# Quantized feed-forward block: scan and down stage in one block, other signed tiles, the first tile in four pieces

## The reference

```python
def act_qdq(x):
    qmax = 2.0 ** (ACT_BITS - 1) - 1.0                     # 32767
    scale = jnp.maximum(jnp.max(jnp.abs(x)) / qmax, 1e-12)  # over the whole tensor
    return jnp.clip(jnp.round(x / scale), -qmax - 1.0, qmax) * scale
...
up = act_qdq(x @ lpbq_dequant(w_up).T)
gate = act_qdq(x @ lpbq_dequant(w_gate).T)
sig = fixed_qdq_u16(jax.nn.sigmoid(gate))
gate = act_qdq(gate * sig)
o = act_qdq(gate * up)
return o @ lpbq_dequant(w_down).T
```

## Time and profile before

| | us |
|---|---|
| median of three runs | 1462.34 |
| profiled execution, its own time | 1460.32 |
| its span on the core | 1458.40 |
| TensorE matmul busy | 1317.7 (90%) |
| VectorE busy | 1034.9 (71%) |
| ScalarE busy | 644.0 (44%) |
| GpSimd busy | 257.4 (18%) |

### The profile page before, as it was taken

The page is one execution under the profiler, slowest core; times in us unless marked ns, Lnnn a source line. Parts: engine busy times, 40 slices in busy tenths (PEclk is TensorE's granted clock), DMA queues, the critical chain, the costliest instruction groups (busy, mean ns, idle before and its releaser), DMA issues. The chain is left out here.

```text
span 1458.4 us, 18728 instructions
## 1 busy us (share of the span) xinstructions
PE 1317.7 (90%) x6142; PEld 1080.4 (74%) x6142; DVE 1034.9 (71%) x1397; ACT 644.0 (44%) x769; POOL 257.4 (18%) x312
## 2 busy tenths in 40 slices
PE   7899999999999979999999899999990039999999
PEld 6678778778878858888888688878880028888887
DVE  0479779868867657777777599999998975454553
ACT  3334334334343233333334255557667963333432
POOL 1024224313313210000000134431210000000000
PEclk9999999999999989999999999999996559999999
DMA  8003212312312456767664889986478853444443
GB/s 317 1 22 116 80 49 88 101 56 69 135 36 103 173 192 229 238 252 239 249 198 155 313 289 319 331 274 216 156 246 356 300 197 115 161 163 156 168 152 114
DMA packets 111240, 259.71 MB, mean 178 GB/s; under 512 B 10832, under 2 KB 23120, under 8 KB 109648
## 3 DMA queue, kind: packets, MB, share of 16 engines
q1 hardware_dynamic: 110896, 259.04, 51.1%
q10 hardware_dynamic: 288, 0.00, 0.0%
HBM read 152.04 MB, written 106.95 MB: 178 GB/s over the span
## 5 line engine op out<-in xcount | busy, mean ns | idle before, releaser
L1141 PE MATMUL gpG<-xph,Wh 128*128 128x512 f32 x384 | 152.8, 398 | 4.3 <-DVE xpl L1065 4.3
L1615 PE MATMUL pD<-Wh,xph 128*128 128x512 f32 x384 | 150.8, 393 | 4.6 <-DVE xpl L1594 4.6
L1141 PE MATMUL pU<-xph,Wh 128*128 128x512 f32 x384 | 150.4, 392 | 1.0 <-POOLq L63 1.0
L1615 PE MATMUL pD<-Wl,xph 128*128 128x512 f32 x384 | 150.5, 392 | 0.0
L1141 PE MATMUL gpG<-xph,Wl 128*128 128x512 f32 x384 | 150.5, 392 | 0.0
L1615 PE MATMUL pD<-Wh,xpl 128*128 128x512 f32 x384 | 150.3, 392 | 0.0
L1141 PE MATMUL gpG<-xpl,Wh 128*128 128x512 f32 x384 | 150.1, 391 | 0.0
L1141 PE MATMUL pU<-xpl,Wh 128*128 128x512 f32 x384 | 149.9, 390 | 0.0
L1141 PE MATMUL pU<-xph,Wl 128*128 128x512 f32 x384 | 149.9, 390 | 0.0
L1594 DVE TENSOR_TENSOR xpl<-doq,xph 128x1536 fp32r<-128x1536 int16 (+1 forms) x34 | 56.4, 1664 | 123.5 <-ACT xph L1561 123.5
L1047 ACT ACTIVATE gst<-gpG,sc 128x512 f32<-128x512 f32 x96 | 66.4, 691 | 165.8 <-PE gpG L1141 165.8
(11 more groups left out here) (172 smaller groups left out, 2863.8 us busy)
## 6 DMA issues: line engine op xcount, KB each, us to landing
dub<-up_d SPq DMA_DIRECT2D x42, 768.0 KB, 4.7
gate_d<-gst SPq DMA_DIRECT2D x96, 256.0 KB, 2.4
gb<-gate_d SPq DMA_DIRECT2D x32, 768.0 KB, 6.5
up_d<-ust SPq DMA_DIRECT2D x96, 256.0 KB, 4.0
xr<-xn_d SPq DMA_DIRECT2D x9, 1024.0 KB, 6.0
xph<-up_d SPq DMA_DIRECT2D x11, 768.0 KB, 6.2
xpl<-up_d SPq DMA_DIRECT2D x11, 768.0 KB, 5.9
xin<-in_x SPq DMA_DIRECT2D x32, 256.0 KB, 2.7
```

The source lines that it names most:

```text
L1141: mm = pe.matmul(ps[:, :], Ws[:, it, kt * P:(kt + 1) * P], xs[:, kt, :], start=(kt == 0 and Ws is Wh and xs is xh), stop=(kt == KT - 1 and ...
L1615: mm = pe.matmul(pD[4 * t + q][:, :], os_[n][:, cs], Ws[:, it, :], start=(it == 0 and os_ is oh and Ws is Wh), stop=(it == IT - 1 and os_ ...
```

## The change

Four things change in down_phase.

1. The scan and the down stage share one block. There is no barrier between them. The buffers of the down stage take over memory of the scan: doq becomes fa, the output rows lie in xui, and the bank for the transpose is the last one of the down stage (pD[7]). SP issues the loads of x behind the last weight load, without a barrier ahead.
2. Tile 0 of the scan is signed.
3. Signed tiles are tile 0 and every third from 2 on: 11 instead of 12.
4. The first down tile is cut into four pieces (256, 256, 512, 512 columns), and VectorE makes two products, then alternates low parts and products. TensorE has one more wait in each of the first three tiles of every four, after half of the first group; ol_done counts four for each tile.

```diff
+            oq = fa
+            yo = [xui[2 + n].bitcast(F32)[:, 0:H] for n in range(2)]
-            pR = pb(ph, "xpR")
+            pD = [pb(ph, f"pD{n}") for n in range(8)]
...
-            def by_act(k):
-                return k % 8 in (0, 2, 3, 5, 6)
+            def signed(k):
+                return k == 0 or k % 3 == 2
...
             def pieces(g):
-                return [(a * 512, (a + 1) * 512) for a in range(3)] if g == 0 else [(0, I)]
+                return [(0, 256), (256, 512), (512, 1024), (1024, I)] if g == 0 else [(0, I)]
...
-                    act.activation(xui[k % NI][:, :], xub[k % NB], ACT.Abs if by_act(k) else ACT.Copy, scale=INV_U).then_inc(xui_done, 1)
-                    if by_act(k):
+                    act.activation(xui[k % NI][:, :], xub[k % NB], ACT.Copy if signed(k) else ACT.Abs, scale=INV_U).then_inc(xui_done, 1)
+                    if not signed(k):
...
                 link(dve.tensor_tensor(C_OUT, S_O, TG_F, ALU.mult))
-            @block.tensor
-            def _(pe):
-                pe.wait_ge(red, 1)
-                everywhere(pe, pR[:, 0:P], T0, ident).then_inc(spread_s, 1)
-
-        with ExitStack() as ph:
-            oq = [sb(ph, f"doq{n}", [P, I], I16) for n in range(2)]
-            yo = [sb(ph, f"dyo{n}", [P, H], F32) for n in range(2)]
-            block = ph.enter_context(nc.Block())
...
-                for g in range(2):
-                    quantize(g)
-                    low(g)
+                quantize(0, (0, 1))
+                for a in range(4):
+                    low(0, (a,))
+                    if a < 2:
+                        quantize(0, (a + 2,))
+                quantize(1)
+                low(1)
...
+                pe.wait_ge(red, 1)
+                everywhere(pe, pD[7][:, 0:P], T0, ident).then_inc(spread_s, 1)
                 with pe.Fori(0, FT // 2) as i:
...
                                 for a in range(3):
-                                    pe.wait_ge(*at(ol_done, 24 * i, 12 * t + 3 * c + a + 1))
-                                    mm = matmuls(t, c, a, range(4))
+                                    if a == 0:
+                                        pe.wait_ge(*at(ol_done, 32 * i, 16 * t + 4 * c + 1))
+                                        matmuls(t, c, a, range(2))
+                                    pe.wait_ge(*at(ol_done, 32 * i, 16 * t + 4 * c + a + 2))
+                                    mm = matmuls(t, c, a, range(2 if a == 0 else 0, 4))
                                 mm.then_inc(d_ps, 1)
```

More of the change, by code:

```diff
@@ L1505, in down_phase @@
             pD = [pb(ph, f"pD{n}") for n in range(8)]
+            xu_in = [*first_u, *(sem(f"x_u_in{n}") for n in range(2, NB))]
+            xui_done, fa_done, p_done, half_done = (sem(f"x_{n}") for n in ("ui", "fa", "p", "half"))
+            pmx_set, apart, link_s, red, spread_s = (sem(f"x_{n}") for n in ("pmx_set", "apart", "link", "red", "spread"))
             x_in = [sem(f"d_x_in{n}") for n in range(2)]
@@ L1510, in down_phase, with upto @@
             block = ph.enter_context(nc.Block())
+            def signed(k):
+                return k == 0 or k % 3 == 2
+            def upto(k, of):
+                return len([q for q in range(k + 1) if of(q)])
             def consumed(g):
@@ L1584, in quantize, with low @@
                     if g >= 2:
-                        dve.wait_ge(ol_done, 3 * (g - 1))
-                    for lo, hi in pieces(g):
+                        dve.wait_ge(ol_done, 4 * (g - 1))
+                    for a, (lo, hi) in enumerate(pieces(g)):
+                        if a not in which:
+                            continue
                         dve.scalar_tensor_tensor(out=oq[n][:, lo:hi], in0=nq[:, g, lo:hi], scalar=C_O,
                                                  in1=ui[n][:, lo:hi], op0=ALU.mult, op1=ALU.mult).then_inc(o_done, 1)
-                def low(g):
+                def low(g, which=range(4)):
                     n = g % 2
                     for a, (lo, hi) in enumerate(pieces(g)):
-                        dve.wait_ge(oh_done, g + 3 if g else a + 1)
+                        if a not in which:
+                            continue
+                        dve.wait_ge(oh_done, g + 4 if g else a + 1)
                         dve.tensor_tensor(ol[n][:, lo:hi], oq[n][:, lo:hi], oh[n][:, lo:hi].bitcast(F32),
-                                          ALU.subtract).then_inc(ol_done, 1 if g == 0 else 3)
-                for g in range(2):
-                    quantize(g)
-                    low(g)
+                                          ALU.subtract).then_inc(ol_done, 1 if g == 0 else 4)
+                quantize(0, (0, 1))
[5 more added lines that the diff above has]
+                low(1)
                 for s in range(QT + 3):
```

84 lines of the change are left out of this document (63 added, 21 removed).

## The result

| | before | changed | ratio, 95% interval |
|---|---|---|---|
| median of 7 runs each | 1461.44 | 1458.18 | 0.9969 [0.9955, 0.9982] |
| timed again, 19 and 12 runs | 1462.60 | 1456.70 | 0.9960 [0.9947, 0.9974] |
| span of the profiled execution | 1458.4 | 1457.4 | |

By the medians the changed kernel is faster by 3.3 us in the first comparison and by 5.9 us in the second. The ratio is taken over all runs and is not the quotient of the two medians, which is 0.9978 in the first comparison (the quotient of the means is 0.9968). The forecast was 1457.5 us and a sum of 4.82 us, which is a ratio of 0.9967; both intervals hold it, and both leave out a ratio of 1. Whether the gain is above the 0.3% that the prediction calls what a measurement can tell is less sure: the ratios stand at 0.31% and 0.40%, and both intervals reach down to less.

What follows compares the result with a forecast made beforehand. TensorE waits 85.9 us for VectorE's scan, so an earlier first down matmul shortens the kernel. 1.38 + 1.72 + 0.49 + 1.23 = 4.82 us off the 1462.34 us median gives 1457.5 us, range 1454.8 to 1461.2.

Steps and rivals of the forecast that it cites:

- Part 1, first tile signed: Scan start: first pass needs only ScalarE's integers, not |f|, and starts 0.28 us after them; gain 1.38 us.
- Part 2, 11 signed tiles: Scan: one pass and one wait for a first half less, two more unsigned pairs; net gain 1.72 us.
- The three prices: VectorE's scan: 1.745 us a pass, 0.265 more per signed tile, 0.145 more per pair of unsigned neighbours.
- The cover of ScalarE: Scan: three tiles cost ScalarE 7.2 us and VectorE 7.4, so VectorE remains the longer one, barely.
- Part 3, one block: Between scan and down stage: without the barrier the first product follows the last scale by 0.20 us; gain 0.49 us.
- The cover of the moved loads: Hand-over: earlier loads can slow tile 1's load of u, but high a stays covered, by 0.6 us at worst.
- Part 4, four pieces: First down tile: first matmul 1.50 us after the first product instead of 2.73; gain 1.23 us.
- The 24 waits: TensorE's down stage: one added wait per tile in three of every four; costed at nothing, at most 0.41 us each.
- The rival that was to end slower: Down stage: TensorE's 24 new waits drain it, up to 0.41 us a place, 1467.3 us at the bound; chance 0.04.
- The slow clock: TensorE's restart: 7 to 14 slow matmuls, 0.20 us more each; 1456.1 us with 7, 1458.7 with 20; no separate chance.
- The rule on semaphores: VectorE's scan: a semaphore costs nothing extra, so the sum would be 4.55 us; the prediction followed the trace's 0.27 instead.
- about 4.8 us earlier than 1190.88: Down stage: when the first matmul was to come, by the clock of the trace.

Runs made afterwards that it cites:

- e5: Changed kernel with tile 0 and every fourth from 3 on signed (9 signed, 41 passes); stretch from ScalarE's first scan conversion to first down matmul 88.27 us, against 84.77.
- e4: Kernel before with its two blocks and barrier kept, but the changed signed order and pieces; 1457.69 us in one run.
- e1: Changed kernel with the first down tile in three pieces of 512 again, all products first; 1459.62 us in one run.
- e6: Changed kernel with 168 more TensorE waits in the down stage; stretch from ScalarE's first scan conversion to first down matmul 84.75 us, against 84.77.
- r3: Changed kernel without an edit, profiled again and timed in five rounds; 1456.70 us against 1462.60 before, ratio 0.9960.

## Why the prediction was right, by its own steps

The forecast was "faster" at 1457.5 us, with a chance of 0.62 and a range of 1454.8 to 1461.2. Both medians, 1458.18 and 1456.70, lie within 1 us of it. That closeness is in part luck: the medians fell by 3.3 and 5.9 us, either side of the sum, and the median of before that the forecast stands on, 1462.34 us of three runs, became 1461.44 with seven. What the runs bear out is the sum, in the stretch. (The prediction once says "all three parts"; it goes on to price all four.)

- **Part 1, first tile signed.** Predicted 1.38 us, measured 1.48. The mis-sized term is small: VectorE starts 0.18 us after a conversion (1107.44 to 1107.62), not the 0.28 us taken over from the pass behind |f|.
- **Part 2, 11 signed tiles.** Predicted 1.72 us and a scan of 79.4 us; measured 1.70 and 79.44. The three prices hold in forms that they weren't taken from: 43 x 1.745 + 11 x 0.265 = 77.95 for 77.90 without pair stalls.
- **The cover of ScalarE.** Predicted 7.2 against 7.4 us for three tiles. e5 put the same sum to 10.06 against 9.28 and found ScalarE deciding. In the changed kernel's own trace the margin stands as ScalarE's one wait in each three tiles, for the buffer of |f|:

```profile
1122.68 1.56 ACT L1497 ACTIVATE xui<-xpl,sc 128x1536 int16<-128x1536 f32 x1
1124.37 1.48 ACT L1501 ACTIVATE xfa<-nq 128x1536 int16<-128x1536 int16 x1
```

The two starts are 1.69 us apart instead of 1.48: 0.21 us, where 0.2 was forecast. With two buffers the |f| so delayed is the one that the pair's 0.15 us on VectorE waits for.

- **Part 3, one block.** Predicted 0.49 us, measured 0.50, and 0.49 by e4. The cover of the moved loads held: ScalarE's conversion of tile 1 ended at 1187.88, and high a started at 1189.71, held only by VectorE's product.
- **Part 4, four pieces.** Predicted 1.23 us and a first matmul 1.50 us after the first product; measured 1.28 and 1.45, and 1.27 by e1. Low a starts 0.97 us after the product, where 1.03 was worked out by straight lines.
- **The 24 waits.** Costed at nothing; measured nothing, and nothing for 168 more (e6). The rival that was to end slower fell.
- **The slow clock.** Predicted as scatter of the run. The 7 to 14 that the prediction names as agreeing were three restarts inside one execution, which can't show a scatter from run to run. The later traces do: the down stage has 14, 14 and 7 slow matmuls in the kernel before and 9 and 8 in the changed one.
- **The rule on semaphores.** By it the sum was 4.55 us; the signed second pass is still 2.01 us behind the first, and a pass that waits for nothing 1.74. The row decided rightly for these passes. No run took the wait out of a signed tile, so the 0.27 us is the distance of passes with and without the wait in one trace.

The sum was 4.82 us and the stretch gave 4.96. The one step that the trace did not bear out as written is "The profiled execution took 1460.32 us ... and would take 1455.5", and with it the sign "about 4.8 us earlier than 1190.88": the first matmul came at 1190.64 in the first trace, and at 1186.80 in r3. That execution of the kernel before was a low one in front of the scan, and the changed kernel's first profiled one took 1459.32. The forecast was safe from this only because it was set against the median of the runs.

## What to carry to other kernels

Compare two traces over the shortest stretch that holds the change, between two named events: here it repeats to 0.02 us, while the spans of one kernel differ by 4 to 5 us for reasons outside. An order that trades one engine's passes for another's should be costed on both engines per period, with the margin written down; the next step beyond it can lose more than the last one gained. A short stall that recurs on a buffer may be bought off with a buffer that the stage can spare elsewhere, as here ten of 0.15 us.

## What the runs showed that was not expected

GpSimd's conversion of 128x1536 took 1.55 us alone and 2.95 us when issued during a VectorE pass with two inputs in SBUF, and the pass queued behind it took 3.09 instead of 1.81 us. Here the third engine was no free help while VectorE was the bound.

In the changed kernel's first trace ScalarE's fourth conversion waited 0.30 us for its load of u, and 0.19 in r3; none of the three traces of the kernel before has such a wait. The prediction had put the loads at nothing. No pass came later for it: the passes around it stand 1.73 to 2.01 us apart as elsewhere.
